# The second block of a two-block vision transformer kernel: three steps moved on VectorE, GpSimd's body written in another order, two copies moved on ScalarE

## What is computed

```python
xn = layernorm(x, g1, b1)
windows, Hp, Wp = window_partition(xn, WS)            # 8 x 8
# attention per window: qkv, softmax(q k / sqrt(16)), times v, projection
x = shortcut + window_unpartition(attention(windows, ...), ...)
h = layernorm(x, g2, b2)
h = gelu(h @ w_fc1 + b_fc1) @ w_fc2 + b_fc2
return x + h
```

## Time and profile before

| | us |
|---|---|
| median of 3 executions (7525.17 to 7528.01) | 7526.51 |
| the profiled execution | 7536.2 |
| its span in the trace | 7534.4 |
| busy: PE / DVE / ACT / POOL | 7125.2 / 6291.5 / 6293.5 / 5480.2 |
| granted TensorE clock, mean | 0.987 |

### The profile page before, as it was taken

The page is one execution under the profiler, slowest core; times in us unless marked ns, Lnnn a source line. Parts: engine busy times, 40 slices in busy tenths (PEclk is TensorE's granted clock), DMA queues, the critical chain, the costliest instruction groups (busy, mean ns, idle before and its releaser), DMA issues. The chain is left out here.

```text
span 7534.4 us, 313308 instructions
## 1 busy us (share of the span) xinstructions
PE 7125.2 (95%) x110894; PEld 5485.8 (73%) x110894; DVE 6291.5 (84%) x13110; ACT 6293.5 (84%) x11444; POOL 5480.2 (73%) x6349
## 2 busy tenths in 40 slices
PE   7999999999999999999999968999999999998998
PEld 4777777777777777777777757777777777777777
DVE  5888888888888888888888857887887887887886
ACT  5999999999999999999999957777777777777776
POOL 3777777777777777777777756776776776776775
PEclk9999999999999999999999979999999999999999
DMA  0111111111111111111111111111111111111111
GB/s 21 30 29 30 30 30 29 29 30 30 30 29 30 30 30 30 29 30 30 30 29 30 29 24 36 41 42 40 41 41 40 41 41 40 41 41 40 42 41 34
DMA packets 379978, 252.67 MB, mean 34 GB/s; under 512 B 284184, under 2 KB 359704, under 8 KB 378520
## 3 DMA queue, kind: packets, MB, share of 16 engines
q1 hardware_dynamic: 378522, 233.09, 12.6%
HBM read 78.64 MB, written 77.07 MB: 21 GB/s over the span
## 5 line engine op out<-in xcount | busy, mean ns | idle before, releaser
L879 POOL TENSOR_TENSOR swin_score<-swin_score,swin_top 113x588 f32<-113x588 f32 x1024 | 1204.6, 1176 | 741.0 <-DVE swin_top L751 740.3
L1546 POOL TENSOR_TENSOR plain_prob<-plain_prob,plain_inv_total 128x384 f32<-128x384 f32 x784 | 635.0, 831 | 671.6 <-DVE plain_inv_total L1459 671.6
L622 ACT ACTIVATE swin_probT<-swin_ps_probs 128x339 f32<-128x339 f32 x2048 | 924.4, 451 | 196.1 <-PE swin_ps_probs L479 176.1
L479 PE MATMUL swin_ps_probs<-swin_ident,swin_prob 113*128 113x113 f32 x6144 | 991.2, 270 | 7.1 <-ACT swin_probT L622 7.1
L479 PEld LDWEIGHTS swin_ps_probs<-swin_ident,swin_prob 113*128 113x128 f32 x6144 | 667.8, 141 | 355.1 <-issue 321.6
L746 DVE TENSOR_TENSOR swin_score<-swin_ps_scores,swin_bias_tab 113x588 f32<-113x588 f32 x1024 | 777.2, 759 | 173.9 <-PE swin_ps_scores L469 172.6
L751 DVE TENSOR_REDUCE swin_top<-swin_score 113x12 f32<-113x588 f32 x1024 | 769.1, 751 | 0.2
L628 ACT ACTIVATE swin_prob<-swin_score 113x588 f32<-113x588 f32 x1024 | 719.2, 702 | 5.8 <-POOL swin_score L879 2.9
L1344 ACT ACTIVATE plain_hid<-plain_ps_dense,plain_b_fc 128x512 f32<-128x512 f32 x588 | 404.3, 688 | 340.1 <-PE plain_ps_dense L1193 322.1
L782 DVE SCALAR_TENSOR_TENSOR swin_x<-swin_y,swin_y_rstd,swin_x_res 98x96 f32<-98x96 f32 x1024 | 603.1, 646 | 0.8 <-POOL swin_y_rstd L897 0.7
L493 PEld LDWEIGHTS swin_ps_mixed<-swin_probT,swin_v_heads 128*32 128x32 f32 x24576 | 422.5, 109 | 223.2 <-issue 145.8
(11 more groups left out here) (185 smaller groups left out, 21081.0 us busy)
## 6 DMA issues: line engine op xcount, KB each, us to landing
swin_k_heads<-swin_k_hat SPq DMA_DIRECT2D x1024, 36.8 KB
plain_x_in<-between_blocks SPq DMA_DIRECT2D x784, 48.0 KB, 2.2
plain_k_heads<-plain_k_hat SPq DMA_DIRECT2D x1176, 32.0 KB, 2.0
out_dram<-plain_x SPq DMA_DIRECT2D x784, 48.0 KB
swin_x_in<-in_x SPq DMA_DIRECT2D x224, 136.5 KB
between_blocks<-swin_x SPq DMA_DIRECT2D x224, 136.5 KB
swin_x_in<-in_x SPq DMA_DIRECT2D x224, 19.5 KB
between_blocks<-swin_x SPq DMA_DIRECT2D x224, 19.5 KB
```

The source lines that it names most:

```text
L479: last = nc.tensor.transpose(psP[:, n * QT:(n + 1) * QT], prob[0:QT, p, 2 * hp:2 * hp + 2, :].rearrange('p h k -> p (h k)'), ident[0:QT, 0 ...
L622: nc.scalar.activation(to, psP[:, 0:3 * QT], ACT.Copy).then_inc(did['probT'], 1)
L879: nc.gpsimd.tensor_tensor(view, view, bcast(top[0:QT, p % 2, :], 2, WIN), ALU.subtract).then_inc(did['shifted'], 1)
L1546: nc.gpsimd.tensor_tensor(pair, pair, bcast(inv_total[0:QT, p // 2, p % 2 * heads:(p % 2 + 1) * heads], 2, WIN), ALU.mult).then_inc(did['p ...
```

## The change

VectorE: `partial_x(3)`, `low_x(2)` and `moments_x(3)` move from the end of the body to a place in front of `residual(-2)`. GpSimd: `power_x` and `norm_x` work on group g + 3 instead of g + 2, and stand behind `residual_x1(-3)` and in front of `scale_probs`, instead of at the start of the body. ScalarE: each of the two `copy_turned(0, p)` stands in front of a `gelu` instead of behind it.

```diff
@@ ScalarE's body @@
                     act.preload_act_table_set(GELU_SET)
+                    copy_turned(0, 0)
                     gelu(-3, 0, B)
-                    copy_turned(0, 0)
+                    copy_turned(0, 1)
                     gelu(-3, 1, A)
-                    copy_turned(0, 1)
                     gelu(-3, 2, B)
@@ VectorE's body @@
                     shift(0, 3)
+                    partial_x(3)
+                    low_x(2)
+                    moments_x(3)
                     residual(-2, B)
                     total(0, 0)
                     low_x1(-3)
...
                     total(0, 1)
                     moments_x1(-2)
-                    partial_x(3)
-                    low_x(2)
-                    moments_x(3)
@@ GpSimd's body @@
-                    power_x(2)
-                    norm_x(2)
                     residual_x(1)
                     power_x1(-3)
                     norm_x1(-3)
                     residual_x1(-3)
+                    power_x(3)
+                    norm_x(3)
                     scale_probs(0, 0)
```

## The result

The changed kernel takes **7612.98 us** at the median of four executions (7612.62 to 7620.44), beside 7525.84 us before. The ratio is 1.0119, with an interval of 1.0101 to 1.0136: 87 us slower. The forecast was 7513 with a range to 7550. It was wrong by its sign.

The account below looks back on a forecast made before the run. The bound was taken as the loop residual, VectorE, moments, GpSimd, x1_res (15.20 us). The new 15.06 plus 0.10 gives 15.16 against 15.24 over 189 groups; with +1.5 us for loop trips and 9.7 off for the median, 7513 us, range 7485 to 7550.

Parts of the forecast that it names:

- Loop N: New loop: scores, shifts, statistics, moments, GpSimd's normalisation, first scaling, TensorE's transposes, next scores; 15.06 us a step.
- The low part: VectorE instruction L1499 with two SBUF inputs; forecast to last 0.69 us instead of 1.35, with GpSimd idle.
- the wait of L1232 for L1546: TensorE's new wait for GpSimd's scaled exponentials, in every group, 0.8 us.
- Rival 1: The low part on VectorE stays at 1.35 us: step 15.78 us, 7628 us; chance 0.05.
- rivals 3 and 4: TensorE's hidden(2) not gated by gelu: 7482 us, chance 0.08; GpSimd's scalings no wait: 7463 us, chance 0.03.
- Loop L: New loop: residual_x, SP's input load, statistics, moments, GpSimd's normalisation, four scalings; 14.70 us at the median landing.
- I add 0.10 per group: Allowance for late input loads on top of Loop N, sized by late DMAs delaying scores: 0.10 us per group.
- Rival 2: Loads landing later by more than 0.36 us make Loop L set the step: 7557 us; chance 0.10.

Follow-up runs that it names:

- e1_early_loads: The changed kernel with x_res in six buffers and residual_x(2), so each load starts a body earlier: 7491.89 us, ratio 0.9949.
- e2_fill_tensor: The changed kernel with TensorE making the product of hidden(-3, 0) twice, loads not moved: 7567.29 us, ratio 1.005.
- e5_early_old_copies: The changed kernel with loads a body earlier and ScalarE's old order of copies and GELUs: 7452.02 us, ratio 0.9901.
- e9_vector_part_early_loads: The kernel before with VectorE's part of the change and loads a body earlier: 7450.89 us, ratio 0.9893.

## Why the prediction was wrong

**What was right.** The bound before (residual, VectorE, moments, GpSimd, `x1_res`) was the loop that I named; with its edges cut and the loads covered the kernel is faster. Loop N was summed at 15.06 and is 15.01 (`e1_early_loads`). The low part at 0.69, the wait of L1232 for L1546 (forecast 0.8, found 0.73) and of L1537 for the moments (about 4, found 4.6) are as forecast, and `hidden(2)` came 1.70 us behind the first transposes, where I had 1.78. Rival 1 was refuted by the row of L1499, rivals 3 and 4 by the step.

**The term that was mis-sized** is the last of "Loop L": "I add 0.10 per group, between 0.02 and 0.35." The loop was found, with 14.70 at the median landing, and its cover is about as worked out: from the end of `residual_x` to the last landing the trace of after has 5.81 us at the median, and VectorE is free for the statistics 6.16 us behind it; group by group, the cover is 0.27 at the median (I had 0.36). But I priced the landings beyond the cover by the 31 late keys of the earlier trace rows, another DMA at another place in the body. Counting the late loads in the trace of before would have given the same price: 39 of 179, with 3.0 us instead of 2.2, are 0.22 x (0.8 - 0.36) = 0.10 us per group. What failed is that landings before the move were taken for landings after it. At its new place the load is late in 66 of 175 groups, with 3.2 us: 0.38 x (1.0 - 0.27) = 0.28. The steps that waited lost 50.4 us, 50.4 / 175 = 0.29 per group. That is inside the bounds that I gave for the term: 15.01 + 0.29 = 15.30, and the time would have been near 7540, inside the range.

**The step that was missing**, and took the time out of the range, is what these waits do to TensorE's clock. TensorE had one idle time of 0.85 us per group before; with covered loads it has 0.30 and 0.74, and with a late load 0.87 and 0.73 (in the group shown), one shortly behind the other, and about every second such group was followed by a fall to half clock. In two of the 33 the clock fell before the second idle time had begun, behind a first one of 1.63 and 1.45 us. The steps with half clock cost 57.1 us over 15.01 (0.33 per group); without the falls some of them would have waited for the load instead, and the net cost is 46 us by `e2_fill_tensor`. I had named the new wait for L1546 and counted its length in N; that it is an idle time behind another one, and what that may cost, was never asked. The Trainium skill ("TensorE: Matmul & The Clock Gate", the section "A second HAM failure mode: psum-queue depth-cycling") tells of a kernel whose clock swings between its levels because TensorE is frequently idle for short times between groups of matmuls. The trace agrees in that the 33 falls away from the trips followed idle times of 0.60 to 1.63 us; but short idle times in every group, 0.30 and 0.74 us, brought no fall in `e1_early_loads`.

**Together** the three kinds add 109.1 / 175 = 0.62 us, and a step is 15.63 us against the forecast 15.16; 0.47 x 189 = 89 of the 100 us between 7513 and 7613. Of the rest, 9.7 us are no cost of the change: the forecast took them off as the distance of the profiled execution from the median, and the profiled execution of the changed kernel, 7612.6, lies at its median. Rival 2 had the direction right (slower through the load). Its price of 7557 left out the clock, and its chance of 0.10 was too small for a case of which the text itself said that nothing hides the landing any more.

**The ScalarE edit** was sized 0.31 us and is 0.225 (`e1_early_loads` against `e5_early_old_copies`). It was rightly seen as a cost in N. It costs nothing in the kernel before, and where N no longer waits for GpSimd it costs nothing either (8 us faster, with overlapping intervals).

## What to carry to other kernels

When an instruction that frees a buffer or reads a load is moved, write down the load's cover before and after, and if the new cover is smaller than the spread of landings, ask how many landings exceed it; the median says nothing, and the count at the old place need not hold at the new one (here 39 of 179 and 66 of 175). Where a kernel has two small idle times on TensorE, a late transfer that lengthens one of them may be charged twice, once as a wait and once as clock. Let a load start a body earlier before tightening the loop in front of it (here by two more buffers for `x_res`, whose making frees the load's buffer): by itself this was worth nothing here, and with the other edits it decided between 87 us slower and 223 us faster.

## What the runs showed of the hardware

**Clock.** Idle times of TensorE of 0.87 us (ended at 6039.72) and 0.73 us (ended at 6041.39) were followed by 3.4 us at 1.2 GHz; idle times of 0.30 and 0.74 us in every group were not, over a whole kernel (`e1_early_loads`). A useless product in the second gap took the falls from 37 to 8 and 46 us from the time.

**Instruction fetches and loads.** Of 105 late landings of two traces, 104 coincide with an instruction fetch in the DMA engines; the late ones take 3.0 us (before) and 3.2 us (after) instead of 2.1 to 2.2. It is a count, and the cause was not tried.

**Two inputs in SBUF.** The low part on VectorE takes 0.69 us while GpSimd idles (after), 1.35 or 1.44 us (`e9_vector_part_early_loads`) when it starts while GpSimd is at work; there it ends 0.54 and 0.55 us behind GpSimd's instruction. By the Trainium skill ("SBUF — State Buffer", "Who interferes with whom") the two lock each other out for whole instructions; the three lengths agree with that.
